# Counting edges in groups of three tiles with three one-hot buffers, and one destination one-hot in each group made by ScalarE

## The reference, cut to what matters

```python
_o = jnp.argsort(dst, stable=True)
src = src[_o]; dst = dst[_o]
...
msgs = feat[src]                                     # L0
neigh = jax.ops.segment_sum(msgs, dst, num_segments=feat.shape[0])
...
scores = jnp.einsum('ehd,ehd->eh', q[src], k[dst])   # L1, softmax over the edges of one source
attn = ex / denom[src]
out = jax.ops.segment_sum(attn[:, :, None] * v[dst], src, num_segments=N)
```

## Time and profile before

| | |
|---|---|
| median of 3 runs | 1731.48 us (1731.39 to 1731.58) |
| the profiled execution | 1731.2 us, its span 1729.3 us, granted clock 0.998 |
| PE busy | 1708.7 us (99%) |
| DVE busy | 1213.0 us (70%) |
| ACT busy | 803.1 us (46%) |
| POOL busy | 557.8 us (32%) |

### The profile page before, as it was taken

How to read it: one execution, slowest core, us unless ns; L and a number is a source line. 1 busy time by engine, 2 the same in 40 slices (tenths; PEclk the granted TensorE clock), 3 DMA queues, 4 the chain that set the end, 5 groups by cost and what they waited for, 6 DMA issues and landing times.

```text
span 1729.3 us, 32333 instructions
## 1 busy us (share of the span) xinstructions
PE 1708.7 (99%) x11894; PEld 1511.5 (87%) x11894; DVE 1213.0 (70%) x2206; ACT 803.1 (46%) x1325; POOL 557.8 (32%) x887
## 2 busy tenths in 40 slices
PE   8999999999999999999999999999999999999998
PEld 7998788889999888889998888899988888999887
DVE  7996569357786875477878673678776835777676
ACT  5667332146665331256663412466644123666531
POOL 1002613313333732023337340133364401333473
PEclk9999999999999999999999999999999999999999
DMA  4003311321111213111113122112131312112222
GB/s 135 2 1 143 123 49 48 123 71 40 47 60 41 93 32 128 40 67 45 46 32 103 50 89 80 46 47 62 32 100 37 107 41 80 33 46 62 68 93 73
DMA packets 64779, 113.08 MB, mean 65 GB/s; under 512 B 15318, under 2 KB 25686, under 8 KB 64640
## 3 DMA queue, kind: packets, MB, share of 16 engines
q1 hardware_dynamic: 64640, 111.22, 19.6%
HBM read 89.19 MB, written 22.00 MB: 64 GB/s over the span
## 4 chain that ended last, share of the span: by engine, by line
PE 96%; DVE 2%; issue 1%; ACT 0%; DVEq 0%; DMA 0%; SPq 0%; POOLq 0%; POOL 0%; ACTq 0%
PE ps L1558 60%; PE ps L1618 16%; PE ps L1713 7%; PE ps L1505 6%; PE ps L1535 3%; PE ps L1645 2%; PE ps L1659 2%; DVE masked_s L1271 1%; DVE pT L1255 0%; DVE w L1426 0%; ACT pT L1022 0%; PE ps L1574 0%; DMA idx_rows<-in_dst_dram 0%; DVE rec_rows L1246 0%; DVEq L426 0%
## 5 line engine op out<-in xcount | busy, mean ns | idle before, releaser
L1255 DVE TENSOR_TENSOR pT<-ps,pT 128x640 fp32r<-128x640 f32 (+1 forms) x320 | 243.9, 804 | 156.3 <-ACT pT L1022 156.2
L1558 PE MATMUL ps<-yT,w 128*128 128x512 f32 (+1 forms) x1728 | 329.9, 352 | 0.0
L1022 ACT CAST pT<-ps 128x640 fp32r<-128x640 f32 (+1 forms) x320 | 202.5, 685 | 254.3 <-PE ps L1713 248.5
L1558 PEld LDWEIGHTS ps<-yT,w 128*128 128x128 f32 x1728 | 280.6, 189 | 44.8
L1558 PE MATMUL ps<-kh,q_parts 128*128 128x512 f32 (+3 forms) x1440 | 310.4, 360 | 7.1 <-DVE small L1271 7.1
L1558 PEld LDWEIGHTS ps<-kh,q_parts 128*128 128x128 f32 (+1 forms) x1440 | 243.0, 186 | 53.4 <-issue 5.9
L1558 PE MATMUL ps<-w,kh 128*128 128x512 f32 (+1 forms) x960 | 235.5, 396 | 0.0
L1618 PE MATMUL ps<-pT,v 128*128 128x256 f32 (+3 forms) x1600 | 215.6, 281 | 0.0
L959 ACT ACTIVATE s<-masked_s,small 128x1250 f32 (+1 forms) x156 | 211.4, 1355 | 0.0
L1558 PEld LDWEIGHTS ps<-w,kh 128*128 128x128 f32 (+1 forms) x960 | 173.7, 186 | 39.1 <-DVE q L1282 1.8
L1618 PEld LDWEIGHTS ps<-pT,v 128*128 128x128 f32 (+1 forms) x1600 | 200.2, 190 | 0.0
(11 more groups left out here) (189 smaller groups left out, 2532.1 us busy)
## 6 DMA issues: line engine op xcount, KB each, us to landing
mask<-mask_dram SPq DMA_DIRECT2D x24, 640.0 KB, 5.0
x_spill<-x SPq DMA_DIRECT2D x36, 256.0 KB
x<-x_spill SPq DMA_DIRECT2D x36, 256.0 KB, 4.3
rep<-rec_dram SPq DMA_DIRECT2D x64, 128.0 KB, 3.3
w_raw<-in_L_gnn_m_w_dram SPq DMA_DIRECT2D x8, 1024.0 KB, 6.6
mask_y<-mask_dram SPq DMA_DIRECT2D x12, 640.0 KB, 5.2
mask_dram<-mask_out SPq DMA_DIRECT2D x10, 640.0 KB, 2.9
w_l<-in_L_gnn_W_dram SPq DMA_DIRECT2D x2, 2048.0 KB, 13.6
```

Source lines behind the costliest of these rows:

```text
L1022: nc.scalar.copy(pT[:, 0, turned_places(gh, half), k * P:k * P + R], turn_bank(half, R)).then_inc(p_high, 1)
L1255: nc.vector.tensor_tensor(pT[:, 1, places, k * P:k * P + R], turn_bank(half, R), pT[:, 0, places, k * P:k * P + R].bitcast(F32), ALU.subtr ...
L1558: mine = mm(to, left(a), right(b), start=first and n == 0, stop=final and n == 2)
```

## The change

`HOT` goes from 4 to 3 and the number of destination one-hots that ACT makes in each group from 2 (written as a number) to `ON_ACT = 1`. So DVE still makes two destination one-hots in each group, of three tiles now and not of four, and the buffer has three places. The constants that round the number of tiles up to whole groups follow `HOT`.

```diff
-HOT = 4
+HOT = 3
+ON_ACT = 1
...
             def dst_hots(j, t, quad):
 
-                for m in range(2):
+                for m in range(ON_ACT):
                     nc.scalar.activation(dst_gap[:, m, :], iota_n[0:ET, j * P:(j + 1) * P], ACT.Abs,
-                                         bias=minus_dst[:, bass.ds(t + HOT - 2 + m, 1)]).then_inc(gap_ready, 1)
+                                         bias=minus_dst[:, bass.ds(t + HOT - ON_ACT + m, 1)]).then_inc(gap_ready, 1)
                 act.wait_ge(hot_used, quad * HOT + HOT)
-                act.wait_ge(gap_ready, quad * 2 + 2)
-                nc.scalar.activation(hot[0:ET, HOT - 2:HOT, NP:NP + P], dst_gap[:], ACT.Relu, bias=1.0,
+                act.wait_ge(gap_ready, quad * ON_ACT + ON_ACT)
+                nc.scalar.activation(hot[0:ET, HOT - ON_ACT:HOT, NP:NP + P], dst_gap[:, 0:ON_ACT, :], ACT.Relu, bias=1.0,
                                      scale=-1.0).then_inc(dst_hot_ready, 1)
...
-            chain(nc.vector.tensor_scalar(beyond, beyond, (LEAST_QUADS - 1) * HOT + 2.5, 1.0 / HOT, ALU.max, ALU.mult))
+            chain(nc.vector.tensor_scalar(beyond, beyond, (LEAST_QUADS - 1) * HOT + 1.0 + (HOT - 1) / 2, 1.0 / HOT, ALU.max, ALU.mult))
...
-                    if m < HOT - 2:
+                    if m < HOT - ON_ACT:
                         nc.vector.tensor_scalar(hot[0:ET, m, NP:NP + P], iota_n[0:ET, j * P:(j + 1) * P],
                                                 edge[:, 1, bass.ds(t + m, 1)], None, ALU.is_equal).then_inc(hot_ready, 1)
...
-                        if m == HOT - 2:
+                        if m == HOT - ON_ACT:
                             pe.wait_ge(dst_hot_ready, q + 1)
```

More of the change, by code:

```diff
@@ L1071, in _ @@
             chain(nc.vector.tensor_reduce(before_end, rel[:, 2, :], AX.X, ALU.min))
-            nc.vector.tensor_scalar(beyond, beyond, 1.0, 1.5, ALU.max, ALU.add)
+            nc.vector.tensor_scalar(beyond, beyond, 1.0, (HOT - 1) / 2, ALU.max, ALU.add)
             chain(nc.vector.tensor_scalar(before_end, before_end, 1024.0, None, ALU.add))
-            chain(nc.vector.scalar_tensor_tensor(first_tile, beyond, -2.5, before_end, ALU.add, ALU.min))
+            chain(nc.vector.scalar_tensor_tensor(first_tile, beyond, -1.0 - (HOT - 1) / 2, before_end, ALU.add, ALU.min))
             chain(nc.vector.tensor_tensor(beyond, beyond, first_tile, ALU.subtract))
-            chain(nc.vector.tensor_scalar(beyond, beyond, (LEAST_QUADS - 1) * HOT + 2.5, 1.0 / HOT, ALU.max, ALU.mult))
+            chain(nc.vector.tensor_scalar(beyond, beyond, (LEAST_QUADS - 1) * HOT + 1.0 + (HOT - 1) / 2, 1.0 / HOT, ALU.max, ALU.mult))
             nc.vector.tensor_scalar(beyond, beyond, ROUND, ROUND, ALU.add, ALU.subtract).then_inc(bounds_ready, 1)
```

## The result

| | before | changed |
|---|---|---|
| median | 1731.48 us (5 runs, 1731.29 to 1731.58) | 1738.33 us (5 runs, 1737.53 to 1738.55) |
| profiled execution, its span | 1731.2, 1729.3 us | 1737.53, 1735.8 us |
| last count matmul over (end of its record) | 127.21 us | 133.80 us |

The ratio is 1.0039 (95% interval 1.0028 to 1.0051), +6.85 us; +5.9 was forecast.

What follows compares the result with a forecast made beforehand. PE's matmuls bounded the kernel; with three places the way over DVE's sequencer would. 18.51 + 2.42 + 7.1 + 102.5 + 1.75 ends at 132.3, plus 0.6 is 132.9 against 127.0: +5.9 us, 1737.4; range 1732.5 to 1740.8.

Steps and rivals of the forecast that it cites:

- PE's work: PE's count matmuls: 186 tiles where there were 196, ten tiles or 5.6 us less for PE.
- DVE's work, 1.71 us a group: DVE's one-hots for a group of three: three sources and two destinations, 1.71 us against PE's 1.675.
- The way from PE to PE over DVE's sequencer: From PE's end of one group over DVE's sequencer back to PE: 2.00 us, making a group 1.87, not 1.675.
- step 3: DVE's loop end, branch, loop head and address steps between register wait and next source one-hot: 1.02 us, none made ahead.
- Rival A: DVE's sequencer steps hide and DVE's own work sets the pace, 1.71 a group: -3.1 us, 1728.4; chance 8%.
- B: PE stays the pace in the counts: -5.6 us, 0.5 of it lost to hitches, 1726.4; chance 3%.
- The short way (C), 1.80: Only the first place's own way from release to reuse binds, 1.80 us a group: +1.6 us, 1733.1; chance 15%.
- ACT at nothing: ACT's copy and Relu at block changes take about 2.2 us, needed after about 2.6: cost put at nothing.
- The start: Second group starts 0.46 us earlier, at 18.51, with PE's clock low until 20.0: about 0.55 more, 2.42 us.
- The term for hitches, 0.6 us: Allowance over the count stretch for DVE's delays, each now reaching PE: 0.6 us, where the old stretch lost 0.35.

Runs made afterwards that it cites:

- head_of_three: Kernel before, each block beginning with three tiles outside the loop, then groups of four with four places going round over all tiles: 1725.66 us, ratio 0.9968.
- half_source: Changed kernel, DVE writing only the first 640 of 1280 columns of each source one-hot, PE reading them twice: 1731.43 us, 1.0002 of the kernel before.
- steps_three: Changed kernel with two more sequencer steps at the end of each turn of DVE's loop: 1743.61 us, 1.0072 of the kernel before.
- three_two: Changed kernel, but ACT makes two destination one-hots in a group (groups of three, three places): 1746.94 us, 1.0089 of the kernel before.

## Why the prediction was right

- **PE's work.** 1860 matmuls, ten tiles less. Right, and head_of_three shows their worth, 5.6 us, once nothing else binds. (The prediction's first paragraph has "what no engine but PE waits for costs nothing"; it has to read: what PE does not wait for costs nothing.)
- **DVE's work, 1.71 us a group.** Right as a bound that does not bind: with 1.2 us of work (half_source) the group was still 1.75.
- **The way from PE to PE over DVE's sequencer.** Right in mechanism and size: 1.02 us for step 3, 1.87 to 1.88 us a group on average in blocks 1 to 5 and 7 to 9. In the blocks single groups differ (1.83 and 1.91 in turn in block 3) and pairs do not, 3.75, as must be where each group waits for the one before the last. That two added steps cost 5.3 us here and nothing with four places is the test by experiment. A second test is in the trace itself: in block 6 the same way is 0.25 us longer (below), and pairs there take 4.00, the whole 0.25 in a pair and half in a group.
- **Rival A.** It falls: steps_three and half_source both show that the loop's steps are not made ahead of the wait. The Trainium skill, "Advanced Engine Details and Errata", Sequencer Loop, has engine instructions wait for semaphores in the queue while others are read. This loop doesn't bear that out, since the step that waits is one of the sequencer's own (L1097 at 46.6 us). No run here tells whether a wait on a constant would sit in the queue instead. The prediction's bound for A and B, a step 3 shorter than 0.8 us, is off: by its own sum two groups at 1.71 leave 3.42 - 1.675 - 0.07 - 0.21 - 0.72 - 0.05 = 0.70.
- **The short way (C), 1.80.** The pairs of 3.75 rule it out as the pace. In block 0, with its shorter loop head, groups take 1.77 to 1.80 us and the two ways are too close to be told apart.
- **ACT at nothing.** Right for the changed kernel, here at a change of block:

```profile
85.98 0.31 ACT L844 ACTIVATE hot<-dst_gap 125x128 bf16<-125x128 f32 x1 [0.33 <-PE ps L1506]
86.61 1.23 ACT L856 COPY counts<-ps 128x1280 f32 x1 [0.32 <-PE ps L1506]
...
88.17 0.31 ACT L844 ACTIVATE hot<-dst_gap 125x128 bf16<-125x128 f32 x1
```

  2.19 us as estimated from the earlier trace rows (2.2). three_two shows what it costs without that room.
- **The start.** Off in two ways that cancel in part. The second group's matmuls began at 18.76, not 18.51: DVE's pause for its registers did not move up by the whole one-hot. And PE's clock was up before it: in the stretches (columns as the earlier trace rows) the first group already ran at 2.4 GHz, where the kernel before had a granted clock of 0.68 from 15.30 to 18.90 us. Why it was up earlier, no run shows; this gain is luck.

```profile
15.30:18.70 3.40, 1.83 (x30) 1.68 (x30) 1.67 (x6) 2.10 (x6) 0.00 (x0) 1.00 1.02 334
18.76:19.95 1.19, 1.19 (x20) 1.13 (x21) 1.19 (x4) 0.26 (x1) 0.00 (x0) 1.00 0.95 244
```

  Together 0.3 us better than the sum.
- **The term for hitches, 0.6 us,** is the one that was too small: it measured about 1.1. All of it lies in block 6, which from its first Relu to that of block 7 takes 14.19 us where seven groups at 1.87 are 13.1:

```profile
87.48 0.55 DVE L1097 TENSOR_SCALAR hot<-iota_n,edge 125x1280 bf16<-125x1280 f16 x1 [0.69 <-PE ps L1506]
...
91.49 0.55 DVE L1097 TENSOR_SCALAR hot<-iota_n,edge 125x1280 bf16<-125x1280 f16 x1 [0.33 <-PE ps L1506]
...
95.48 0.55 DVE L1097 TENSOR_SCALAR hot<-iota_n,edge 125x1280 bf16<-125x1280 f16 x1 [0.32 <-issue]
```

  Two groups take 4.01 and 3.99 us there and not 3.75. The same hitch was in the kernel before, in block 5, where the slack hid all but some 0.3 us of it (Relus 2.88 us apart at its start, 2.58 at the other blocks'). The rest of the difference, PE through at 133.6 and not at 132.9, is spread over the groups: 1.87 us also at the blocks' starts, for which the sum took 0.04 off, and 0.1 more in block 0.
- **What stays open.** The profiled execution is the fastest of the five; the others are 0.7 to 1.0 us longer, and no trace shows where. By the profiled ones alone the change costs 6.3 us. What makes block 6 slower is open too.

## What to carry to other kernels

A ring of buffers has to be long enough for the whole way from the consumer's release back to the consumer, and the sequencer's steps are on it: register steps, loop end, branch and loop head that stand behind a wait on a register are not made ahead of it, as DVE's loop shows here. Sum that way (here 2.00 us against 2.23 with four places, 1.675 with three) before taking a place out, and look for it in start-to-start distances, since overlapping records can show neither engine idle. Where fewer wasted tiles are what is wanted, split the group's size from the ring's length: a short head outside the loop gained 5.6 us where the smaller group with its shorter ring lost 6.9.

## What the runs showed of the hardware

- In one block DVE's loop turns more slowly. The steps of the changed kernel's loop, once in block 6 (90.2 to 91.05 us) and once in block 2 (46.6 to 47.2 us), by the source views of L1097 and L1111:

```profile
L1097 DVEq FUSED_REGOPS  x1: 57/57/57, 90.2 to 90.2; - x1
L1111 DVEq COMPARE_BRANCH  x1: 56/56/56, 90.7 to 90.7; - x1
L1111 DVEq FUSED_REGOPS  x2: 82/142/202, 90.5 to 91.0; - x2
...
L1111 DVEq COMPARE_BRANCH  x1: 56/56/56, 46.9 to 46.9; - x1
L1111 DVEq FUSED_REGOPS  x2: 79/137/195, 46.7 to 47.1; - x2
```

  From the waited step to the loop end it is 0.26 us and not 0.13, and from the branch to the loop head 0.31 and not 0.19. Together the way from the waited step to the next source one-hot is 91.49 - 90.21 = 1.28 us in this turn and 1.02 in block 2 (1.57 in the first turn of block 6, 1.26 to 1.28 in those between). Branches of 0.30 us are in block 5 of the kernel before and in block 3 with the head of three. The block changes with the code and the input doesn't, which speaks for the place of the loop's code; no run moves the code alone. The Trainium skill, "Runtime: NRT & Kernel Launch", Instruction fetch mechanics, has a taken branch to code outside the fetched pages wait for a fetch; whether it is that, no row here shows.
- DVE waited for PE 27.7 us of 108 and was still what PE waited for (half_source). Where both sides of a ring wait for each other in turn, as here, the ring is too short for the way.
